# Routed experts and a ternary feed-forward layer on one core: a reordered first stage and a drain of its own for the last tiles

## The reference

```python
x = x + tanh(g_xattn[0]) * experts(layernorm(x), ids, C, C, C)
x = x + tanh(g_ffn[0]) * ffn(layernorm(x), w_gate, w_up, w_down)

def experts(h, ids, Wg, Wu, Wd):              # per expert e: silu(h Wg'[e]) * (h Wu'[e]), times Wd'[e]
def ffn(x, w_gate, w_up, w_down):
    gate = bitlinear(x, w_gate); up = bitlinear(x, w_up)
    return bitlinear(fwht(silu(gate) * up), w_down)
def bitlinear(x, w):  return act_quant(x) @ weight_quant(w).T
def weight_quant(w):  s = 1 / clip(mean(abs(w)), 1e-5); return clip(round(w * s), -1, 1) / s
def act_quant(x):     s = 128 / clip(max(abs(x), -1), 1e-5); return clip(round(x * s), -128, 127) / s
```

## Time and profile before

| | |
|---|---|
| median of 3 runs | 460.95 us |
| the profiled execution | 458.56 us |
| its span (first to last instruction) | 456.8 us |
| mean granted clock of TensorE | 0.977 of full speed |
| busy: PE / DVE / ACT / POOL | 394.6 / 379.4 / 286.0 / 197.4 us |

### The profile page before, as it was taken

The page is one execution under the profiler, slowest core; times in us unless marked ns, Lnnn a source line. Parts: engine busy times, 40 slices in busy tenths (PEclk is TensorE's granted clock), DMA queues, the critical chain, the costliest instruction groups (busy, mean ns, idle before and its releaser), DMA issues.

```text
span 456.8 us, 7541 instructions
## 1 busy us (share of the span) xinstructions
PE 394.6 (86%) x2170; PEld 272.6 (60%) x2171; DVE 379.4 (83%) x650; ACT 286.0 (63%) x438; POOL 197.4 (43%) x215
## 2 busy tenths in 40 slices
PE   1067889999999979599999999999999999996772
PEld 0055667776777744265666666666666666665530
DVE  5782488768967977899999999999999999987660
ACT  6315436665485463356978788778878887877500
POOL 0687012202212133446556665765586567342110
PEclk9999799999999999989999999999999999999987
DMA  8787023402520000023623552453345244526631
GB/s 313 270 290 244 19 90 106 174 0 92 184 93 1 1 11 13 11 46 59 104 64 85 107 114 47 103 116 92 67 104 117 64 85 105 117 45 106 122 85 47
DMA packets 51142, 44.68 MB, mean 98 GB/s; under 512 B 44848, under 2 KB 44848, under 8 KB 49072
## 3 DMA queue, kind: packets, MB, share of 16 engines
q1 hardware_dynamic: 46256, 27.63, 21.9%
q0 software_dynamic: 4864, 16.78, 15.6%
HBM read 21.33 MB, written 4.19 MB: 56 GB/s over the span
## 4 chain that ended last, share of the span: by engine, by line
PE 59%; DVE 14%; POOL 9%; issue 7%; DMA 5%; ACT 2%; DVEq 1%; SPq 1%; POOLq 0%; ACTq 0%
PE bank L420 12%; PE bank L479 10%; PE bank L486 10%; PE bank L503 10%; PE bank L510 10%; PE bank L392 6%; POOL xs L287 2%; POOL item_var L295 2%; DMA xs<-x_dram,order 1%; DVE prod L1019 1%; DVE ymax_part L999 1%; DMA mixed<-mixed 1%; POOL item_rstd L298 1%; DVEq L841 1%; DMA xqT<-xq 1%
## 5 line engine op out<-in xcount | busy, mean ns | idle before, releaser
L503 PEld LDWEIGHTS bank<-cst,mT 128*128 128x128 f32 x512 | 66.3, 191 | 15.4 <-issue 4.6
L503 PE MATMUL bank<-cst,mT 128*128 128x128 f32 x512 | 68.2, 276 | 4.8 <-ACT mT L665 4.8
L479 PE MATMUL bank<-wq,xqT 128*128 128x512 bf16 x256 | 67.5, 387 | 4.4 <-DMA xqT<-xq 3.6
L510 PE MATMUL bank<-wq,yqT 128*128 128x512 bf16 x256 | 66.6, 387 | 3.6 <-DMA yqT<-yq 3.6
L486 PE MATMUL bank<-wq,xqT 128*128 128x512 bf16 x256 | 67.2, 386 | 0.5 <-DVE prod L1019 0.5
L295 POOL TENSOR_SCALAR item_var<-item_mv 128x1 f32<-128x1 f32 x19 | 14.1, 741 | 88.9 <-DVE item_mv L851 88.7
L690 ACT ACTIVATE sg<-bank,gate_s 128x512 f32<-128x512 f32 x64 | 43.8, 684 | 13.9 <-PE bank L479 12.1
L665 ACT ACTIVATE mT<-bank 128x512 f32<-128x512 f32 x64 | 38.0, 593 | 21.7 <-PE bank L392 21.6
L375 POOL DMA_INDIRECT out_dram<-res,order x16 | 19.5, 1221 | 72.8 <-DVE res L1039 69.2
L1019 DVE TENSOR_TENSOR prod<-bank,sg 128x512 f32<-128x512 f32 x64 | 43.3, 677 | 7.0 <-PE bank L486 6.6
L653 ACT ACTIVATE y<-y,yqs 128x512 int8<-128x512 f32 x56 | 40.2, 718 | 12.3 <-POOL yqs L342 12.3
(11 more groups left out here) (134 smaller groups left out, 871.3 us busy)
## 6 DMA issues: line engine op xcount, KB each, us to landing
mixed<-mixed POOLq DMA_DIRECT2D x16, 512.0 KB, 5.3
stage<-ctx_dram SPq DMA_DIRECT2D x4, 1024.0 KB, 8.0
stage<-wgate_dram SPq DMA_DIRECT2D x4, 1024.0 KB, 4.7
stage<-wup_dram SPq DMA_DIRECT2D x4, 1024.0 KB, 4.7
stage<-wdown_dram SPq DMA_DIRECT2D x4, 1024.0 KB, 4.7
yqT<-yq SPq DMA_TRANSPOSE x64, 2.4
cst<-consts_dram SPq DMA_DIRECT2D x1, 338.0 KB, 3.0
xs<-x_dram,order POOLq DMA_INDIRECT x16, 4.3
```

Of the source, the lines that this page charges most:

```text
L479: last = nc.tensor.matmul(ps_gate[:, :], xqT[:, b, c, :], wq[:, 0, c * F + 512 * n:c * F + 512 * (n + 1)], start=(c == 0), stop=(c == DC - 1))
L503: last = nc.tensor.matmul(bank_[:, c * P:(c + 1) * P], mT[:, n % 2, c, :], had, start=True, stop=True)
L510: last = nc.tensor.matmul(ps_down[b][:, :], yqT[:, m, g, :], wq[:, 2, block_ * D:(block_ + 1) * D], start=(m == 0 and g == 0), stop=(m == ...
```

## The change

**Start.** The gate values get a semaphore of their own, so PE and DVE no longer wait for that DMA. The comparison that makes the row picks is done in two halves, and the pick matmuls follow each half. The first low part of the expert matrices (`ct_lower(0)`) moves behind the tables. 49 matmuls whose result nobody reads (`spin`) stand on PE: 24 ahead of the first statistics, 5 ahead of the first transposes, 6 ahead of the first product and 14 ahead of `a_transposes(0)`. The 16 gathers are divided among the POOL work otherwise: 4, then two scales, 2, a scale, 4, a scale, 4, a scale, 2.

**First stage.** On DVE both clip passes of a chunk stand together at the end of an item, and `update` stands ahead of `normalise`. The rounds are written out on DVE and ACT (tile numbers below 13 are then constants). ACT rounds the last chunk of a matrix one item later, and the last chunk of all after `body(0)`.

**End.** `body(16)` and `tail()` go, and `drain()` comes. In it DVE does only three butterfly levels for tile C. For each quarter of C's transform PE adds two products: one half times the Hadamard matrix and the other half times it or its negative (`neg_had`). The integers of B and C are shared by DVE and ACT, and the scales of A are made on DVE.

```diff
@@ SP: turn_y @@
-                if t >= NT - 2:
-                    sp.wait_ge(yq_end_set, (t - (NT - 2)) * NQ + (m + 1))
+                if t == NT - 2:
+                    sp.wait_ge((yq_end_set, yq_end_act)[m // 2], m % 2 + 1)
+                elif t == NT - 1:
+                    sp.wait_ge((yq_end_set, yq_end_act)[m % 2], 2 + m // 2 + 1)
@@ POOL @@
             n = item_scale(0, n)
+            n = item_scale(1, n)
             gather(4)
-            n = item_scale(1, n)
-            for t in range(5, 8):
+            gather(5)
+            n = item_scale(2, n)
+            for t in range(6, 10):
                 gather(t)
-            n = item_scale(2, n)
-            for t in range(8, NT):
+            n = item_scale(3, n)
+            for t in range(10, 14):
                 gather(t)
-            for k in range(3, NI):
+            n = item_scale(4, n)
+            for t in range(14, NT):
+                gather(t)
+            for k in range(5, NI):
@@ PE @@
+            def spin(count):
+                for _ in range(count):
+                    nc.tensor.matmul(bank[7][:, :], spin_w, spin_x, start=True, stop=True)
...
+            spin(24)
+            pe.wait_ge(stats_set, 1)
+            spin(5)
             x_transposes(0, 0)
+            spin(6)
             pe.wait_ge(tables_set, 1)
             up_product(0, 0, first=True)
             x_transposes(1, 1)
+            spin(14)
             a_transposes(0)
...
+            def last_hadamard(p):
+                first = 2 * (p // 2)
+                upper, lower = (first + 2) % NQ, (first + 3) % NQ
+                pe.wait_ge(mT_set, (NT - 1) * NQ + first + 2)
...
+                for c in range(4):
+                    nc.tensor.matmul(end_had[p % 2][:, c * P:(c + 1) * P], mT[:, upper, c, :], had, start=True, stop=False)
+                    last = nc.tensor.matmul(end_had[p % 2][:, c * P:(c + 1) * P], mT[:, lower, c, :],
+                                            had if p % 2 else neg_had[:, :], start=False, stop=True)
...
+            def drain():
+                mix(0)
+                mix(1)
+                down_product_int(Z, Z % 2, 1)
+                had_b(0)
+                down_product_int(Z, Z % 2, 2)
+                had_b(1)
+                mix(2)
+                mix(3)
+                down_product_int(Z, Z % 2, 3)
+                had_b(2)
+                had_b(3)
+                for p in range(2):
+                    last_transposes(p)
+                down_product_int(A, A % 2, 0)
+                last_hadamard(0)
+                for p in range(2, 4):
+                    last_transposes(p)
+                down_product_int(A, A % 2, 1)
+                last_hadamard(1)
+                down_product_int(A, A % 2, 2)
+                for p in range(2, 4):
+                    last_hadamard(p)
+                down_product_int(A, A % 2, 3)
                 for t in (B, C):
@@ ACT @@
+                integers(A, 2)
+                integers(A, 3)
+                last_evacuate(2)
+                last_evacuate(3)
+                last_y(0)
+                last_y(1)
+                end_integers(B, 2, 0)
+                end_integers(B, 3, 1)
+                last_y(2)
+                last_y(3)
+                end_integers(C, 1, 2)
+                end_integers(C, 3, 3)
@@ DVE: an item of the first stage, and the drain @@
+                    act_mul(k)
...
+                        x_lower(k + 1, 1 - b)
...
+                        stats(k + 2, b, s, tau_next)
+                    update(k - 1, tau=tau_update)
+                    if more:
+                        dve.wait_ge(item_done, k)
+                        normalise(k + 2, b, tau_next)
+                    if not (last and i == 5):
+                        a_lower(k)
...
+                        s.did(ts(stage[:, c, :], stage[:, c, :], wscale[:, ds(w)], 1.0, ALU.mult, ALU.min))
+                        s.wait()
                         ts(stage[:, c, :], stage[:, c, :], -1.0, MAGIC, ALU.max, ALU.add).then_inc(wclip_set, 1)
...
+                for m in range(2):
+                    y_integers(B, B % 2, m)
+                finish(Z, Z % 2)
+                for p in range(NQ):
+                    if p == 2:
                         finish(A, A % 2)
+                    dve.wait_ge(y_set, C * NQ + p + 1)
+                    n = LAST_ORDER[p]
+                    step = st.did(nc.vector.tensor_reduce(ymax_part[:, c, p:p + 1], y[:, c, 512 * n:512 * (n + 1)],
+                                                          AX_X, ALU.max, apply_absolute_value=True))
+                end_scales(C, step, NQ)
+                dve.wait_ge(yqs_set, C + 1)
+                for m in (0, 2):
+                    y_integers(C, c, m)
                 finish(B, B % 2)
+                finish(C, c)
```

More of the change, by code:

```diff
@@ L1142, in _ @@
             st.n += (NT - 6) * per
-            for t in range(NT - 2, NT + 1):
+            for t in range(NT - 2, NT):
                 body(t, t % 2, st, **flags(t))
-            tail()
+            drain()
 def constants():
```

313 lines of the change are left out of this document (186 added, 127 removed).

## The result

The changed kernel takes 441.82 us (median of 4 runs, 440.22 to 443.05) against 460.47 us (4 runs, 458.59 to 462.06). The ratio is 0.9595, 95% interval 0.9542 to 0.9647. Forecast were 442 us and a range of 437 to 450.

The account below looks back on a forecast made before the run. Both stages were taken as PE-bound, the first with 16.4 us of holes, and the end as a chain over a DMA. Terms -2.4 - 14.1 + 1.0 + 0 - 3.3 = -18.8 us gave 439.8 profiled, 442 us median, range 437 to 450.

Parts of the forecast that it names:

- The items: First stage, 16 item intervals: holes of 16.4 us shrink to 2.3, from 119.3 to 105.2 us, a gain of 14.1.
- POOL's late answer: Clip items: POOL's small operations wait for the lower clip, so `normalise` starts 0.72 us after DVE is free.
- the 7 us that I had named for clip items: Sign against the forecast: item intervals with a clip at 7 us or more.
- The start: Up to `up_product(1)`: earlier row order, faster first gather, shorter DVE row; from 33.31 to 30.9 us, a gain of 2.4.
- The 24 products: Start, lower bound: 24 spins at the slow rate take 11 us, end at 22.5 past the first transposes; gain 0.
- From the last items to tile 0: From `up_product(17)` to tile 0's gate products: both clips ahead of `act_mul(18)` make 17.6 of 16.6 us, a loss of 1.0.
- The tiles: Tile 0's body: DVE's wait of about 1 us for ACT's last rounding is offset; 0, bounds -1 and +1.5.
- The drain: End of kernel: C's summing DMA leaves the chain, doubled Hadamard products add 3.56 us; a gain of 3.3 us.
- The last two maxima did wait for `finish(A)`: Sign against the forecast, in the drain: the last maximum of y waits for `finish(A)` alone.
- The gathers still stall: Rival, first items: the 0.8 us margin is missing and two items lose 2 us each; 446 us, chance 0.08.
- POOL's answer holds DVE: Rival, clip items: DVE needs 7.4 us an item and bounds the first stage; 449 us, chance 0.13.
- The low clock: Rival, first stage: PE stays at 1.2 GHz, each product costs 2.7 us more; 469 us with ten, chance 0.03.

Follow-up runs that it names:

- Experiment 1: The kernel before with only the new division of the 16 gathers among the POOL work: 455.79 us, ratio 0.9879 to the kernel before.
- Experiment 2: The changed kernel with the old DVE order of clips, normalise and update in items 3 to 5 of a round: 448.16 us, ratio 0.9718.
- experiment 3: The kernel before with only the new drain: 454.34 us, ratio 0.9863 to the kernel before.
- experiment 11: The changed kernel with ACT's pick factor earlier, `ct_lower(3)` later, item 17's clip pair behind tile 0's quantising, and tile 14's store held: 437.13 us, ratio 0.9533.
- Experiment 7: The changed kernel with `ct_lower(3)` behind `act_mul(0)` and `x_lower(1)` on DVE instead of ahead of them: 440.43 us, ratio 0.963.
- Experiment 8: The changed kernel with item 17's clip pair behind tile 0's quantising and `finish(A)` behind the last tile's integers on DVE: 439.95 us, ratio 0.9612.
- experiment 9: The changed kernel again, unedited, as a control: 441.34 us, ratio 0.9646 to the kernel before.
- Experiments 6 and 10: The changed kernel with the last tile's old fourth level: in 6 its adding DMA stands behind a store, 449.88 us; in 10 ahead of it, 444.11 us.
- Experiment 5: The changed kernel with all integers of the last two tiles on DVE, none on ACT: 442.48 us, ratio 0.966.
- experiment 4: The changed kernel without its 49 unread spin matmuls: 444.29 us, ratio 0.9628 to the kernel before.

## Why the prediction was right, and where it was not

The mechanisms came as laid out in the items, at tile 0 and in the drain. That the median lies within 0.2 us of the forecast is luck. By the profiled executions the change is worth 15.9 us (458.56 to 442.68) and not 18.8. The 2.9 us too few are mostly the start (1.9), the tiles (0.8) and the items (0.5), less 0.4 at tile 0. And the median of the changed kernel is 0.9 below its profiled execution, where the forecast had it 2.4 above. These two misses, 2.9 and 3.3 us, cancel.

- **The items (14.1 forecast, 13.6 measured).** Right in mechanism and size. The stall went whole. Experiment 1 shows that the new gathers alone bring 5.8 us net, because they then meet `ct_lower`. In the changed kernel the row of three starts at 23.91, and so does the last gather of that group: it isn't held and takes 1.03 us. Experiment 2 shows 5.0 us for the order of the clips in the items and 1.1 behind them. ACT's order in the items changed as well (its wide passes moved from ahead of silu to behind `x_upper`), and PE's small matmul moved behind `a_transposes`. Neither was tried alone; of the 6.2 us that the items gained beside the stall, experiment 2 leaves 1.3 for them. I had named both parts: DVE's 7.1 us work in a clip item, and POOL's late answer. The answer is quicker than laid out, since POOL's small operation falls from 1.07 to 0.19 us when no clip runs. The holes that are left are 16 x 6.43 short of 105.69, so 2.8 us (2.3 forecast), and 2.4 of them are the three intervals with the weights' matmul. I had put them down to DVE's lag, but PE waits for nothing of DVE there. These three, at 7.15 to 7.26 us, reach the 7 us that I had named for clip items as a sign of being wrong; the other intervals with a clip do not.
- **The start (2.4 forecast, 0.5 measured).** The term that was mis-sized most. About 1.0 of the difference is a DMA: the first chunk, issued at the same 2.12 us, landed at 7.1 before and 9.5 after. Seven more profiles have the changed order of the start; in the two where it landed at 7.03 and 7.10, `up_product(1)` is at 31.79 and 31.67. The old start has it at 33.31, and at 33.00 in experiment 3, with landings at 7.11 and 7.16. So the edit is worth 1.3 to 1.6 us. The late chunk counts since ACT's pick factor stands behind its first pass; in experiment 11, where it doesn't, a landing at 9.17 does no harm. The missing 0.8 is the statistics and `normalise` that I took out from among the three `ct_lower`: from `normalise(0)` to `up_product(1)` it was 11.38 us and is 11.43. `x_lower(0)` now stands ahead of the three, and DVE waits 0.30, 0.44 and 0.34 us there. Experiment 7 shows that the row of three is what holds PE. The 24 products did not become the bound: nine of them were 0.43 us apart and the rest 0.22, and they ended at 19.6 us. The sentence in the Trainium skill that I weighed ("SBUF — State Buffer", "Who interferes with whom") infers that such a subtraction and descriptor generation don't meet. Gather 3 took 2.31 us beside `ct_lower(0)` as I had laid it out, and experiment 1 adds two of 2.60 and 2.42. The inference does not hold for these gathers. They also read the order of the rows from SBUF, and no run here tells apart which part of a gather is held.
- **From the last items to tile 0 (1.0 lost forecast, 0.6 measured).** Right in kind: PE idle twice, 1.74 us (2.1 laid out) and 2.35. Experiment 8 takes it away: 15.28 us.
- **The tiles (0 forecast, 0.8 lost).** One interval is 16.48 us instead of 15.67, behind an x transpose that landed late (4.1 us after its issue). It is not in every execution: in experiment 9 it does not occur, and the stretch is 234.2 us. Five of the eleven profiles with the new first stage have it; what brings it stays open. I had priced ACT's last pass from a clip on DVE, 1.2 to 1.3 us. It takes 1.90, and DVE waits 0.79 us for it.
- **The drain (3.3 forecast, 3.3 measured).** Each point came where it was laid out, measured from the end of tile C's third level: last down product of tile A 13.3 us behind it (13.5 laid out), end of the first quarter of integers 17.2 (17.5). In my layout the PE work from 419.8 adds up to 432.1 and not to 432.4, so by its own terms it gave 3.6. The last two maxima did wait for `finish(A)`, which I had named as a sign of being wrong, but the layout already had `finish(A)` and both maxima behind A's last down product. Experiment 8 shows what taking it away brings to the scales: 1.5 us. Experiments 6 and 10 show that the DMA was worth removing, at twice the matmuls, and that 1.9 of the 3.3 us hang on it. Experiment 5 confirms that sharing the integers brings 0.3 us at most.
- **The rivals.** "The gathers still stall" and "POOL's answer holds DVE" did not happen, but experiments 1 and 2 show their mechanisms at work when half the change is missing. The low clock came in no item: it is at 1.00 from 30 to 140 us. It came at the end, in some executions on the last eight products, for 1.7 us, which no case of mine had. The page of the Trainium skill on the clock gate ("TensorE: Matmul & The Clock Gate", "Part 1: The HAM clock gate") says that activity releases PE's clock. That spoke for the 49 products at the start, and the traces agree: item 0's matmuls are 0.23 us apart with them and 0.43 without.

By the stretches the parts add up: 5.8 (gathers) + 6.1 (clips) + 3.3 (drain) + 0.5 (start) = 15.7 of the 16.1 us that the span lost. The medians give 4.6 + 6.3 + 6.1 = 17.0 of 18.65, but 2.8 of the drain's 6.1 are not in its stretch, so that sum is no check.

## What to carry to other kernels

Cost an instruction with what runs beside it, not by its best row: here a GpSimd operation that started under a long VectorE subtraction or clip ended only behind it (2.13 us in place of 0.19), so the short operation that others wait for belongs behind the long one or well ahead of it. Before an experiment on a DMA, write down what stands ahead of it on its queue. When transfers end a kernel, keep stores out of their way, even at the price of issuing a store later. And before you read a clock from a view, see that the trace has an entry there, and check it by the distance between two matmuls.

## What the runs showed of the hardware that was not expected

- **POOL beside DVE.** An indirect gather takes 1.0 to 1.2 us alone, and 2.3 to 3.1 if it starts under a `ct_lower` of DVE (two of 2.91 and 3.06 are in the kernel before). The edge is sharp: one that started 0.01 us behind a `ct_lower` took 1.03, one 0.08 us behind took 3.06. A one-column `tensor_scalar` takes 0.19 us alone, 1.07 to 1.11 if it starts under a clip pass and 2.13 under `ct_lower`. The gathers ended 0.9 to 1.1 us behind the DVE instruction, the `tensor_scalar` 0.05.
- **A DMA transpose beside other DMAs.** At the end it lands 2.4 us after its issue alone, 2.6 and 3.5 us beside one indirect store (the chain of the changed kernel, 426.49, has the 3.5), 5.06 beside two, and 4.39 beside the adding DMA.
- **The first loads.** With the same issue times the first context chunk landed between 7.03 and 9.49 us in the fourteen profiles.
- **The clock after a wait.** After 3 us of waiting the granted clock fell to 0.50 in both executions compared in experiment 4, but not at the same product. In one the eight right behind the wait took 3.26 us and the last eight 1.90. In the other it fell later, and the last eight took 3.59. What decides between the two was not settled.
- **The clock at the start.** After 9.57 us without a matmul the first four transposes took 1.09 us and item 0's matmuls were 0.43 us apart (experiment 4). Behind the unread products it was 0.66 and 0.23. The kernel before has 0.43 as well, and 4.46 us from the first start of item 0's product to the last.
